# Attention and expert-mixed projection on one core: mask table loaded a batch sooner, all row maxima masked on VectorE, and the last steps reordered

## What is computed

```python
x = x + layernorm(attention(layernorm(x)))
x = x + layernorm(ffn(layernorm(x)))
# attention: 32 query heads, 8 key/value heads, head_dim 32, rotary, causal
scores = where(causal, q @ k.T / sqrt(32), -1e20); out = softmax(scores) @ v; return out @ w_o.T + b_o
# ffn: a base projection 1024 x 1024 plus the two best of 8 rank-16 updates, weighted by a softmax
weights, selected = top_k(x @ gate_w.T, 2)
result = x @ base_w.T + base_b + 2.0 * sum_e w_full[e] * (x @ lora_A[e].T) @ lora_B[e].T
```

## Time and profile before

| what | value |
|---|---|
| median of 3 runs without the profiler | 1037.3 us (1036.18 to 1037.53) |
| the profiled execution's own time | 1043.99 us |
| its span, first to last instruction | 1042.3 us |
| mean granted PE clock, share of 2.4 GHz | 0.988 |
| PE busy | 1008.5 us, 97% |
| DVE, ACT, POOL busy | 61%, 38%, 43% |

### The profile page before, as it was taken

The page is one execution under the profiler, slowest core; times in us unless marked ns, Lnnn a source line. Parts: engine busy times, 40 slices in busy tenths (PEclk is TensorE's granted clock), DMA queues, the critical chain, the costliest instruction groups (busy, mean ns, idle before and its releaser), DMA issues.

```text
span 1042.3 us, 17345 instructions
## 1 busy us (share of the span) xinstructions
PE 1008.5 (97%) x6414; PEld 823.2 (79%) x6414; DVE 638.7 (61%) x1882; ACT 400.9 (38%) x682; POOL 452.3 (43%) x492
## 2 busy tenths in 40 slices
PE   6999999999989998999999989999999999999995
PEld 6888898898876665666666559999999999999995
DVE  6753533334447886788888747666666666666654
ACT  6331221200126775777777754222222222222221
POOL 1453443523337986899998851111111111111110
PEclk9999999999989998999999999999999999999998
DMA  9342431246236766656555455222222222222101
GB/s 356 138 143 102 146 132 66 91 146 178 81 135 175 205 186 161 162 138 172 141 138 138 121 176 170 79 81 83 82 87 80 84 80 74 84 82 79 53 21 40
DMA packets 78787, 127.29 MB, mean 122 GB/s; under 512 B 7792, under 2 KB 47088, under 8 KB 75632
## 3 DMA queue, kind: packets, MB, share of 16 engines
q1 hardware_dynamic: 78704, 126.19, 40.4%
HBM read 85.27 MB, written 40.37 MB: 121 GB/s over the span
## 4 chain that ended last, share of the span: by engine, by line
PE 92%; DVE 3%; DMA 2%; POOL 1%; ACT 1%; issue 0%; SPq 0%; POOLq 0%; DVEq 0%; ACTq 0%
PE bank L1272 21%; PE bank L1274 21%; PE bank L1273 20%; PE bank L1345 8%; PE bank L1371 7%; PE bank L1387 7%; DMA q_t<-shift_l 2%; PE bank L1281 2%; PE bank L1407 2%; PE bank L1529 1%; PE bank L1413 1%; PE bank L1410 1%; DVE bank L1015 1%; DVE ln_st L953 1%; POOL ln_rs L655 0%
## 5 line engine op out<-in xcount | busy, mean ns | idle before, releaser
L1015 DVE CUSTOM_DVE_ANT_0 bank<-bank,row_mask 128x128 f32<-128x128 f32 (+1 forms) x480 | 219.5, 523 | 61.1 <-PE bank L1345 57.1
L655 POOL TENSOR_TENSOR ln_rs<-ln_ve,minus_half 128x1 f32<-128x1 f32 x64 | 61.5, 961 | 394.6 <-DVE ln_mm L958 394.6
L837 ACT ACTIVATE prob<-bank 128x512 f32<-128x512 f32 x320 | 173.8, 598 | 44.8 <-PE bank L1371 44.7
L1272 PE MATMUL bank<-wf_h,xt_h 128*128 128x384 f32 (+1 forms) x384 | 129.7, 338 | 1.8 <-DVE z L1178 1.8
L1274 PE MATMUL bank<-wf_l,xt_h 128*128 128x384 f32 (+1 forms) x384 | 130.2, 339 | 0.0
L1273 PE MATMUL bank<-wf_h,xt_l 128*128 128x384 f32 (+1 forms) x384 | 129.6, 338 | 0.0
L1345 PE MATMUL bank<-k_t,q_t 96*128 96x384 f32 (+3 forms) x512 | 126.1, 343 | 3.0 <-DVE row_top L1015 3.0
L1272 PE MATMUL bank<-xt_h,wq_h 128*128 128x512 f32 x304 | 120.5, 397 | 0.0
L1274 PE MATMUL bank<-xt_l,wq_h 128*128 128x512 f32 x304 | 118.7, 390 | 0.0
L1273 PE MATMUL bank<-xt_h,wq_l 128*128 128x512 f32 x304 | 118.5, 390 | 0.0
L1371 PE MATMUL bank<-q_t,k_t 98*128 98x512 f32 x320 | 113.3, 418 | 5.2 <-DMA q_t<-shift_l 4.6
(11 more groups left out here) (118 smaller groups left out, 1944.8 us busy)
## 6 DMA issues: line engine op xcount, KB each, us to landing
q_t<-q_scratch SPq DMA_DIRECT2D x32, 512.0 KB, 5.3
q_scratch<-turn_h SPq DMA_DIRECT2D x16, 512.0 KB, 2.7
q_scratch<-turn SPq DMA_DIRECT2D x16, 512.0 KB, 2.9
q_t<-q_scratch SPq DMA_DIRECT2D x32, 256.0 KB, 5.5
att_scratch<-att SPq DMA_DIRECT2D x32, 256.0 KB, 2.4
at_raw<-att_scratch SPq DMA_DIRECT2D x16, 512.0 KB, 3.9
x<-x SPq DMA_DIRECT2D x16, 512.0 KB, 4.2
out<-z SPq DMA_DIRECT2D x15, 512.0 KB, 2.9
```

Source lines behind the costliest of these rows:

```text
L655: nc.gpsimd.tensor_tensor(ln_rs[j][:], ln_ve[j][:], minus_half[:], ALU.pow).then_inc(count, 1)
L837: nc.scalar.activation(prob[n % 2][:, i, :, :].rearrange("p h q -> p (h q)"), bank[3 + (NS * n + i) % 3][:], ACT.Exp, scale=INV_SQRT_HD).t ...
L1015: last = nc.vector.tensor_tensor_reduce(out=row, in0=row, in1=row_mask[:, SEQ - w:SEQ], scale=1.0, scalar=LOWEST, op0=ALU.add, op1=ALU.max ...
L1272: mm(dst, a_h, w_h, start=start, stop=False, skip_group_check=True)
```

## The change

- `row_mask` moves to the last 2 KB per partition of region C, behind slots 0 to 2, which are free as soon as batch 2 has been projected. SP loads it then, ahead of the four first `load_group`.
- All groups are masked on DVE. The mask matmuls (22), `ident_r`, `causal_r`, their load and their two copies go; a semaphore wait moves to the first `denominators`.
- The score banks turn by one place, so S0 and S1 of group 0 no longer wait for the last value bias on DVE.
- SP: bias row bo in step 9, bf in step 11, the first FFN chunk in step 13; the inverses are stored in steps 13, 21 and 29 and taken on DVE in 12, 20 and 28.
- Step 30: DVE takes the shift ahead of `split_att(0)`, ACT does its half of `split_att(0)` after exps 5, and PE does S7 before O0, S8 before O1 and S9 before O2.
- Last group: the add that joined two key blocks for D is left out and the last four D matmuls get 256 columns instead of 128. x of tile 0 is loaded ahead of FFN chunk 3. DVE waits for POOL's second norm instruction instead of its first in two places, and some splits trade places with `normalise_x1`, `transposed2` and `lo2`.
- Last tile: `lora_ps` and `z_step` are counted per column block; ffn(15) may start when block 0 of the tile before is out, and PE does blocks 0 and 1 of ffn, the low part, lora 0 and 1, and then ffn and lora of block 2. DVE takes the sums and the first half of the statistics as blocks come.

```diff
-ORDER_OUT = [("S0 S1 S2 V0 V1 V2 V3 T S3 S4 S5 D S6 O0 S7 O1 S8 O2 S9 O3 "
-              "O4 O5 O6 O7").split(),
+ORDER_OUT = [("S0 S1 S2 V0 V1 V2 V3 T S3 S4 S5 D S6 S7 O0 S8 O1 S9 O2 "
+              "O3 O4 O5 O6 O7").split(),
...
             if s == SLOTS - 1:
+                row_mask = m("row_mask", [P, SEQ])
                 m = Map(e_at + SPILL, e_size - SPILL)
...
-        row_mask = Map(m.at)("row_mask", [P, SEQ])
...
+        def score_bank(n, i):
+
+            return bank[3 + (NS * n + i + 1) % 3]
...
                     if b == BATCH - 1 and p == 0:
+                        sp.wait_ge(proj_ps, 2 * USES * (BATCH - 1))
+                        sp.dma_start(row_mask[:], row_mask_h).then_inc(mask_loaded, 16)
                         for n in range(SLOTS):
                             load_group(n)
...
-            sp.wait_ge(proj_ps, PROJECTED)
-            sp.dma_start(row_mask[:], row_mask_h).then_inc(mask_loaded, 16)
...
-                if n >= KV and n % KV == 2:
+                if n >= KV and n % KV == 5:
                     store_inverses(n // KV - 1)
...
-                if n == WO_LOADS:
+                if n == WO_LOADS + 1:
                     sp.dma_start(bo_row[:], b_o[0].partition_broadcast(P)).then_inc(late_loaded, 16)
+                if n == WO_LOADS + 3:
                     sp.dma_start(bf_row[:], b_ffn[0].partition_broadcast(P)).then_inc(late_loaded, 16)
-                if n == WO_LOADS + 2:
+                if n == WO_LOADS + 5:
...
+            load_res(0)
             sp.wait_ge(score_ps, NS * NG)
             load_ffn(3)
             sp.dma_start(before[:], before_h[0].partition_broadcast(P)).then_inc(late_loaded, 16)
-            load_res(0)
...
                 mask(n, 3)
                 if n == NG - 1:
                     scale_y(0)
-                add_keys(n, 2, total[:, 1, :, :], None, SCORES.index((2, 3)))
                 if n < NG - 1:
+                    add_keys(n, 2, total[:, 1, :, :], None, SCORES.index((2, 3)))
...
-                if n == NG - 2:
-                    split_att(0)
...
                 exps(n, 5)
+                if n == NG - 2:
+                    split_att(0)
...
             split_ffn(3)
+            normalise_x1(0)
             copy_sums(NG - 1)
+            transposed2(0)
             split_ffn(4)
-            normalise_x1(0)
             split_ffn(5)
-            transposed2(0)
...
+                if n == 0 and i == 0:
+                    dve.wait_ge(mask_loaded, 16)
                 dve.wait_ge(row_ps, NR * n + i + 1)
...
-                    nc.vector.tensor_reduce(row_top[n % 2][:, heads[0]:heads[-1] + 1, qb],
...
                 for b, (at, w) in enumerate(FFN_COLS):
                     lo = max(at, AGW)
+                    if t == NT - 1 and b == 2:
+                        dve.wait_ge(z_step, s + 2)
+                        nc.vector.bn_stats(ln_st[1][:, 0, :], z[:, 0:HALF]).then_inc(z_step, 1)
+                    dve.wait_ge(lora_ps, 3 * t + b + 1)
...
-            dve.wait_ge(y_scale, 1)
+            dve.wait_ge(y_scale, 2)
             split_att(1)
             split_ffn(2)
             residual1(0)
-            dve.wait_ge(y_scale, 3)
+            dve.wait_ge(y_scale, 4)
             split_ffn(3)
-            split_ffn(4)
             project_bias(1, 0)
             lo2(0)
+            split_ffn(4)
...
-                diagonal = dst[:, 0:len(heads) * w].rearrange("p (h k) -> p h k", k=w)[:, :, P * qb:w]
-                mm(diagonal, ident_r[:], causal_r[:].unsqueeze(1).broadcast_to([P, len(heads), P]), start=False,
-                   stop=True, skip_group_check=True).then_inc(row_ps, 1)
...
-                pe.wait_ge(prob_summed, SUMS * n + (SUMS if n < NG - 1 else 3))
+                pe.wait_ge(prob_summed, SUMS * n + (SUMS if n < NG - 1 else 2))
...
+            ffn(NT - 1, (0, 1))
             transpose_low(NT - 1)
-            lora(NT - 1)
+            lora(NT - 1, (0, 1))
+            ffn(NT - 1, (2,))
+            lora(NT - 1, (2,))
```

More of the change, by code:

```diff
@@ L1009, in maxima @@
                     wait(dve, shift_ps, n - 1)
-                if masked_later(n, i):
-                    if n == 2:
-                        dve.wait_ge(mask_loaded, 16)
-                    for at, h in enumerate(heads):
-                        row = row_bank(n, i)[:, w * at:w * at + w]
-                        last = nc.vector.tensor_tensor_reduce(
-                            out=row, in0=row, in1=row_mask[:, SEQ - w:SEQ], scale=1.0, scalar=LOWEST,
-                            op0=ALU.add, op1=ALU.max, accum_out=row_top[n % 2][:, h, qb:qb + 1])
-                    last.then_inc(row_max, 1)
-                else:
-                    nc.vector.tensor_reduce(row_top[n % 2][:, heads[0]:heads[-1] + 1, qb],
-                                            row_bank(n, i)[:, 0:len(heads) * w].rearrange("p (h k) -> p h k", k=w), AX_X, ALU.max
-                                            ).then_inc(row_max, 1)
+                for at, h in enumerate(heads):
+                    row = row_bank(n, i)[:, w * at:w * at + w]
+                    last = nc.vector.tensor_tensor_reduce(
+                        out=row, in0=row, in1=row_mask[:, SEQ - w:SEQ], scale=1.0, scalar=LOWEST,
+                        op0=ALU.add, op1=ALU.max, accum_out=row_top[n % 2][:, h, qb:qb + 1])
+                last.then_inc(row_max, 1)
             def shift_lo(n):
@@ L1179, in ffn_sum @@
                                             ).then_inc(z_step, 1)
-                dve.wait_ge(z_step, s + 3)
-                statistics(z, 1, z_step, s + 3)
+                if t == NT - 1:
+                    dve.wait_ge(z_step, s + 4)
+                    nc.vector.bn_stats(ln_st[1][:, 1, :], z[:, HALF:D]).then_inc(z_step, 1)
+                    moments(1, z_step, s + 3)
+                else:
+                    dve.wait_ge(z_step, s + 3)
+                    statistics(z, 1, z_step, s + 3)
             def residual2(t):
@@ L1203, in _ @@
                 maxima_of(0, 1, 2)
+                if n + 1 < NG:
+                    shift_lo(n + 1)
                 if n == NG - 2:
                     split_att(0)
-                if n + 1 < NG:
-                    shift_lo(n + 1)
                 maxima_of(3, 4, 5)
-                if n >= KV and n % KV == 2:
+                if n >= KV and n % KV == 4:
                     invert_sums(n // KV - 1)
@@ L1417, in denominators @@
                         dst = den_bank(n)[HD * h:HD * h + HD, :].rearrange("p (b q) -> p b q", q=P)
-                        last = mm(dst[:, 2:3, :], ones[:], p[:, FIRST[2]:FIRST[2] + 1, h, :], start=False, stop=True,
+                        last = mm(dst[:, 2:4, :], ones[:], p[:, FIRST[2]:FIRST[2] + 2, h, :], start=False, stop=True,
                                   skip_group_check=True)
@@ L1531, in transpose2, with ffn @@
                 last.then_inc(xt2_ps, 1)
-            def ffn(t):
-                wait(pe, z_step, 9 * (t - 1) + 3)
-                for b, (at, w) in enumerate(FFN_COLS):
+            def ffn(t, blocks=range(3)):
+                for b in blocks:
+                    at, w = FFN_COLS[b]
+                    wait(pe, z_step, 9 * (t - 1) + b + 1)
                     for i, c in enumerate(FFN_ORDER):
@@ L1548, in transpose_low, with lora @@
                 nc.tensor.transpose(bank[7][:, 0:P], low[:].rearrange("p e r -> p (e r)"), ident[:]).then_inc(low_ps, 1)
-            def lora(t):
+            def lora(t, blocks=range(3)):
                 pe.wait_ge(low_ready, t + 1)
-                for b, (at, w) in enumerate(FFN_COLS):
+                for b in blocks:
+                    at, w = FFN_COLS[b]
                     lo = max(at, AGW)
@@ L1556, in lora @@
                                    False, True)
-                last.then_inc(lora_ps, 1)
+                    last.then_inc(lora_ps, 1)
             project_out(1, 0)
```

37 lines of the change are left out of this document (14 added, 23 removed).

## The result

| | before | after |
|---|---|---|
| median without the profiler, same chip | 1036.7 us (1035.2 to 1037.5) | 1023.0 us (1021.6 to 1023.2) |
| profiled execution, time | 1044.0 us | 1021.6 us |
| its span | 1042.3 us | 1019.8 us |
| mean granted PE clock | 0.988 | 0.998 |

The medians differ by 13.8 us. The ratio is 0.9857, with a 95% interval of 0.9837 to 0.9878, which is 12.6 to 16.9 us. The 1023.0 is inside the range (1012.8 to 1026.0), but 6.9 us above the predicted 1016.1, and outside the range that the forecast gave itself (1013.5 to 1019). The sum of 21.2 us fits the profiled execution, whose span is 22.5 us shorter, and not the median. Most of the experiments are about those 7 to 9 us.

The account below looks back on a forecast made before the run. PE, busy 97% of the span, was taken as the bound, with its waits and low clock behind them. Terms 2.8 + 6.5 + 7.5 + 2.1 + 2.3 = 21.2 us, from 1037.3, gave 1016.1 us; range 1012.8 to 1026.0.

Parts of the forecast that it names:

- step 3: Attention loads spread over more steps: the late shift's stall at step 9 goes, 7.5 us, between 0.3 and 7.8.
- step 4: Steps 30 to 32 and tile 0: key_sum wait and slow stretch go, new waits come; 2.1 us, between 0.5 and 3.5.
- step 5: Last tile by column blocks: ffn starts sooner and less work follows the last sum; 2.3 us, between 1.5 and 2.6.
- Step 1: Primed units: mask matmuls leave PE, 3.0 us, less 0.2 of lateness of the first row unit; 2.8 us.
- Step 2: Change-over to attention: no wait for the mask, the shift's DMA is next late; 6.5 us, between 2.5 and 7.3.
- This reordering makes a new wait: Step 30: PE waits about 1.1 us for DVE before O0, and the step ends 0.7 us later.
- The shift stall of step 9 is the profiled execution's own: Rival: timed runs have no such stall, so spreading the loads gives 0.5 us; 1023.1 us, chance 0.22.
- The clock falls at one new wait: Rival: a slow stretch follows S0 of step 1, O0 or tile 1's transposes, costing 3.5 to 6 us; 1019.6 to 1022, chance 0.17.
- The loads are only moved: Rival: shifts of steps 10, 12 and 14 land 1 to 2 us late, spreading gains about 3; 1020.6 us, chance 0.08.
- Slower: Rival: PE's clock stays low over step 0, the O matmuls and tile 0, costing 26 us; 1042 us, chance 0.03.
- nothing: Rival: DVE paces PE in step 0 and the mask was not the cause; 1035.3 to 1039.3 us, chance 0.02.
- a gain in the profiled execution of over 5 us more than in the median: Sign named in advance that the prediction is wrong: the profiled gain exceeds the median's gain by over 5 us.

Follow-up runs that it names:

- versions 1 and 2: version 1, and the same with GpSimd instead of VectorE making the low part of the last FFN chunk; the latter 1017.7 us, ratio 0.9789 to the kernel before.
- version 1: Kernel after with ACT's split half after exps 3, three last-block FFN chunks before lora, first output weights behind group 1's shift; 1020.0 us, ratio 0.9810 to the kernel before.

## Why the prediction was right, and where it was off

**The bottleneck and the places were right.** By the sum, PE's waits and what its clock does behind them are the gain but for 3.0 us of masks and 1.5 us of DVE's shorter end of the last tile. Stretch by stretch, the profiled execution gained what the sum says: 21.2 predicted, 22.5 measured, of which 1.0 is a start that varies.

**What was off is the price of the stalls, and it entered by one sentence: "I subtract the same microseconds from the median."** Steps 2 to 4 were priced by pitches of one execution, and that execution had the longest stretches at 1.2 GHz of all profiles with those waits, and the longest wait for the shift. The forecast's own range, 1013.5 to 1019, missed for this reason. The stated range held because it had been stretched to the rival without the stall, and in that it owes something to luck: the stall did exist.

This is step 9 in each of the profiles with the loads together. The excess is the pitch from T of step 9 to T of step 10, less 9.18; the loss by the clock is the length of the window times (1 - PEclk):

| profile | wait for the shift | window, PEclk | loss by the clock | wait + loss | excess |
|---|---|---|---|---|---|
| before, first | 3.72 | 7 us, 0.51 | 3.4 | 7.1 | 7.2 |
| before, again | 2.37 | 4 us, 0.57 | 1.7 | 4.1 | 4.3 |
| only the mask's place | 2.87 | 4 us, 0.57 | 1.7 | 4.6 | 4.85 |
| only steps 30 to 32 | 3.15 | 4 us, 0.59 | 1.6 | 4.8 | 5.1 |
| after, loads together | 2.22 | 4 us, 0.57 | 1.7 | 3.9 | 4.1 |
| VectorE masks | 1.93 | none | 0 | 1.9 | 2.2 |
| only the last tile | 1.04 | none | 0 | 1.0 | 1.3 |

Wait and clock together explain the excess within 0.3 us every time; both vary. The median excess over the seven profiles is 4.3 us, and the differences of medians of the timed experiments are 4.5 and 5.5. The 7.2 is the largest of the seven, but three of the seven profiles are of the fastest or second fastest execution of their kernel, so the 4.3 may be low.

The granted clock recorded with every timed execution carries this further. The 66 executions of the kernel before beside the experiments have 0.986 to 0.996, with a median of 0.991; 13 of them have 0.988, the value of the execution that was read, or less. These 13 have a median of 1042.4 us, the 27 with 0.992 or more one of 1037.9. The 14 executions of the kernel after have 0.996 to 0.999, with a median of 0.998. One less the clock, times the span, is 9.3 us before and 2.0 after: some 7 of the 14 to 16 us gained are clock. In the pair of profiled executions it is 12.5 and 2.0. So the execution read had about 3 us more of low clock than a typical one, and three of the 66 took as long as it did or longer.

Step by step, by the timed parts, with the terms of the sum beside them:

| part | predicted | measured, by the medians | by the interval |
|---|---|---|---|
| steps 1 and 2, masks and change-over | 9.3 | 7.4 | 5.5 to 11.4 |
| step 3, loads spread | 7.5 | 5.5 alone, 4.5 inside after | 4.7 to 9.1 alone |
| step 4, steps 30 to 32 | 2.1 | 0.8 | -0.8 to 2.9 |
| step 5, last tile | 2.3 | 2.8 | 1.2 to 4.9 |
| sum | 21.2 | 16.5 | |

Each term lies inside the interval of its own part. What shows that the sum was too high is the whole change, the run with the loads together (for step 3), the mask's place alone (whose 6.6 us of the earlier trace rows are excluded), and the profiles. The whole change measured 16.1 us by the medians (14.2 to 19.5) in the set that also had the first and the third of these parts, and 13.8 and 15.3 in the other two comparisons; the 21.2 is outside all three intervals. The kernel before moved most: its median was 1036.7 in the first comparison and 1038.5 to 1040.6 in the sets, while the kernel after had 1022.4 to 1023.6 every time.

- **Step 1 (masks off PE)** held. From the first row unit to T of step 0 it is 67.63 us before and 63.78 after. The 3.85 are the forecast's 3.0 of masks and 0.85 by S0 and S1; the 0.2 of lateness didn't come. No run has the turned banks without the masks, so the split between the two is by the sum. No primed row unit waited for DVE.
- **Step 2 (change-over)** had the right mechanism and the right next wait. The size was off, by the clock: 15.54 to 9.87 us in the pair of profiles compared above, but 12.4 to 12.9 in the four other profiles with the mask late, and 9.6 to 9.9 in the six with it early and no masks on PE (8.9 in versions 1 and 2, which issue the first output weights later).
- **Step 3 (loads spread)** as in the table. Spreading did not only move the stall: the slowest shift of after landed in 3.4 us. The step was mis-sized in both of its factors, the wait (3.72 us, against 1.04 to 3.15 in the other profiles) and the low clock behind it.
- **Step 4** was right in its parts. "This reordering makes a new wait" is shown by the run with the old order: the reordering loses 1.0 to 1.2 us where 0.7 was forecast. The 2.1 us of the stretch has to be read with the clock: where no low clock followed the key_sum wait, the old order took 54.07 or 53.55 us, so the new one wins 1.0 or 0.4.
- **Step 5** was right: 2.2 us in the profiles of after and of the last tile alone.

**The rivals.** "The shift stall of step 9 is the profiled execution's own" gave 1023.1, and 1023.0 was measured. The number agrees by luck, and the reason is half right: the stall is in every profile with the loads together, and taking it away alone gains 5.5 us where this rival had 0.3 to 0.5. What was the execution's own is the excess length at step 9 and at step 0 alike. The prediction looked at the 6.7 us of excess and asked which one stall might be missing in the other runs; against the second profile, 2.9 of it stood at each of two stalls. "The clock falls at one new wait": no profile that has one of the new waits shows a low clock behind it. "The loads are only moved" would have left shifts of steps 10, 12 and 14 late by 1 to 2 us; the pitches from step 9 to 14 after are 9.2 to 9.4. Two other profiles show a little of it: 9.8 behind step 10 in the run with step 30 in its old order and 9.6 in version 1, with 9.7 behind step 14 in both, 0.4 to 0.6 us over the regular pitch. The slowest shift took 4.6 to 7.1 us with the loads together and 3.2 to 3.9 with them spread. The Trainium skill (DMA: Bandwidth & Descriptors, "Queues, rings and completion order") has each DMA engine take its descriptors in ring order. Those landing times agree with it: with less issued ahead of it, the slowest shift lands sooner. "Slower" and "nothing" are out.

One sign named in advance as "wrong" did appear, "a gain in the profiled execution of over 5 us more than in the median": 22.5 against 13.8. It points at the profiled execution, which is where the error lay, and not at one of the places of the change.

Three things stay open. Why the clock stays low for 4 us in one execution and 10 in the next after the same wait is not settled; no run varied that alone. Nor is it settled why the shift's wait at step 9 ranges from 1.0 to 3.7 us with the same loads ahead of it. And of step 4, the timed gain of the last denominators by themselves, without the reordering, was not measured apart.

## What to carry to other kernels

A wait that drops PE's clock has no single price: here the wait for key_sum cost from nothing to 1.7 us on top of itself, and the one for the mask from 1.7 to 5.2. Before pricing it by a pitch, read the same stall in a second profile or price it as the wait plus half of a stretch whose length is uncertain; compare the granted clocks of the timed executions, and take an execution that lies 6 us over its median as the upper bound. Taking such waits away also narrows the scatter, here from 6.4 to 9.3 us within a set (9 to 29 executions) to 1.3 to 3.6 (4 to 6 executions). And when steps are reordered to cover one wait, compute who is late in the new order: undoing that one reordering, and later beating it with an earlier split, gave 1 to 2 us that the change had left.

## What the runs showed that I had not expected

- The length of the 1.2 GHz stretch isn't a property of the wait. After 2.88 us for key_sum, the same in six profiles that keep the old order of the last steps, the clock was low for 3 to 4 us in four of them and not at all in two. After 2.3 to 2.6 us for the mask it was low for 4, 7, 7, 7 and some 10 us. From attention on, no profile shows a low clock behind a wait of PE of 1.93 us or less (the last microseconds, when PE has no work left, apart); behind the waits of 2.2 us and more one came every time but those two.
- GpSimd makes the 128x1160 subtraction in 3.25 us, against 1.3 on DVE (5.20 for four), and DVE's bias (0.68 us) and statistics (1.29 for two) at that time kept their length. The product that DVE starts as GpSimd ends took 1.33 us instead of 1.22.
